# The slot loop of a hypergraph layer: four pairs of row banks, the next round's first tiles and gates made in this round, two tiles scaled on ScalarE

## The reference

```python
h = x @ W
beta = sigmoid((h @ a_gn)[:, None, :] + (agg @ a_ge)[:, :, None])
all_he = beta[..., None] * h[:, None, :, :] + (1.0 - beta[..., None]) * agg[:, :, None, :]
all_he = elu(all_he)
logits2 = where(H[None, :, :] > 0, se[:, None, :], NEG)
coefs1 = softmax(logits2, axis=-1)
g = einsum('bne,benf->bnf', coefs1, all_he)
```

## Time and profile before

| | |
|---|---|
| time, median of 3 runs | 2310.97 us (2310.77 to 2312.5) |
| profiled execution | 2305.04 us, of which the span is 2303.3 |
| VectorE busy over the span | 2034.9 us, 88% |
| TensorE matmuls | 2041.7 us, 89% |
| ScalarE | 1391.4 us, 60% |
| GpSimd | 929.2 us, 40% |
| the loop's first VectorE instruction starts at | 130.65 us |
| the next part starts at | 322.34 us |
| rounds of the loop | 9 (72 adds on GpSimd, 8 a round) |

### The profile page before, as it was taken

The page is one execution under the profiler, slowest core; times in us unless marked ns, Lnnn a source line. Parts: engine busy times, 40 slices in busy tenths (PEclk is TensorE's granted clock), DMA queues, the critical chain, the costliest instruction groups (busy, mean ns, idle before and its releaser), DMA issues. The chain is left out here.

```text
span 2303.3 us, 61385 instructions
## 1 busy us (share of the span) xinstructions
PE 2041.7 (89%) x26444; PEld 1347.3 (58%) x26444; DVE 2034.9 (88%) x2731; ACT 1391.4 (60%) x2174; POOL 929.2 (40%) x534
## 2 busy tenths in 40 slices
PE   6888866478878699999999999999999999998886
PEld 5654534345566466666666666666666666665654
DVE  7568866589757599999999999999999999999995
ACT  4422222389731466667766667766677766676784
POOL 2259950145400234444444444444444444432221
PEclk9999978678979799999999999999999999999998
DMA  3000000334300421021121211201210210123442
GB/s 126 1 0 0 0 0 1 75 62 78 48 2 1 93 53 38 30 57 39 30 47 39 52 35 39 52 25 39 52 43 30 43 43 30 34 57 60 71 71 47
DMA packets 176819, 94.74 MB, mean 41 GB/s; under 512 B 158552, under 2 KB 163864, under 8 KB 176432
## 3 DMA queue, kind: packets, MB, share of 16 engines
q1 hardware_dynamic: 176560, 90.94, 18.1%
HBM read 80.09 MB, written 10.83 MB: 39 GB/s over the span
## 5 line engine op out<-in xcount | busy, mean ns | idle before, releaser
L603 ACT ACTIVATE x_sb<-x_sb,hid_neg_max 128x1024 f32<-128x1024 f32 x576 | 661.7, 1154 | 289.7 <-DVE hid_neg_max L518 289.5
L527 DVE STREAM_TRANSPOSE hid_weights_t<-x_sb 128x1024 f32<-128x1024 f32 x576 | 712.2, 1237 | 2.7 <-ACT x_sb L603 2.3
L518 DVE CUSTOM_DVE_ANT_0 x_sb<-ps_score,adj_mask,row_scale 128x1024 f32<-128x1024 f32 x512 | 638.9, 1248 | 16.4 <-PE ps_score L386 15.3
L406 PE MATMUL ps_low<-hid_weights_t,hid_x_rep 32*64 32x256 f32 x18432 | 573.3, 382 | 11.5 <-ACT hid_share L633 11.1
L386 PE MATMUL ps_score<-hid_y_hi,hid_xs 128*128 128x512 f32 x1152 | 522.0, 453 | 34.9 <-DVE hid_neg_max L518 29.4
L406 PEld LDWEIGHTS ps_low<-hid_weights_t,hid_x_rep 32*64 32x64 f32 x18432 | 390.8, 132 | 168.4 <-issue 97.6
L386 PE MATMUL ps_score<-hid_y_lo,hid_xs 128*128 128x512 f32 x1152 | 456.6, 396 | 0.0
L713 POOL TENSOR_TENSOR hid_z<-hid_z,hid_inv_cols 128x1024 f32<-128x1024 f32 x64 | 194.5, 3040 | 553.9 <-ACT hid_z L611 553.9
L386 PEld LDWEIGHTS ps_score<-hid_y_hi,hid_xs 128*128 128x128 f32 x1152 | 217.0, 188 | 261.7 <-issue 151.1
L386 PEld LDWEIGHTS ps_score<-hid_y_lo,hid_xs 128*128 128x128 f32 x1152 | 218.4, 190 | 43.9 <-issue 15.0
L705 POOL TENSOR_TENSOR hid_y_wide<-hid_y_wide,hid_y_hi 128x1024 f32<-128x1024 f32 x64 | 153.6, 2400 | 191.5 <-ACT hid_y_wide L594 191.5
(11 more groups left out here) (350 smaller groups left out, 3058.8 us busy)
## 6 DMA issues: line engine op xcount, KB each, us to landing
hid_inv_cols<-hid_inv_rows SPq DMA_DIRECT2D x64, 512.0 KB, 3.7
hid_x_rep<-hid_row_space SPq DMA_DIRECT2D x64, 256.0 KB, 5.8
gat_x_rep<-gat_row_space SPq DMA_DIRECT2D x32, 256.0 KB, 5.7
gat_e_wide<-gat_e_space SPq DMA_DIRECT2D x8, 512.0 KB, 6.5
marks<-hid_mark_rows SPq DMA_DIRECT2D x8, 512.0 KB, 4.8
x_sb<-in_x SPq DMA_DIRECT2D x4, 512.0 KB, 5.8
hyp_neighbours<-in_adj SPq DMA_DIRECT2D x4, 512.0 KB, 7.1
edge_adj_high<-in_adj SPq DMA_DIRECT2D x4, 512.0 KB, 9.0
```

The source lines that it names most:

```text
L406: ins = pe.matmul(m.ps_low[c * F:(c + 1) * F, a, 0:NT * Q], x_rep[a * Q:(a + 1) * Q, batch_of(g) % 2, b, :], weights_t[a * Q:(a + 1) * Q, ...
L518: dve.tensor_tensor_reduce(ring[:, i % RING, :], m.ps_score[:, i % 2, :], mask, scale, HUGE, ALU.add, ALU.min, neg_max[:, g % 2, t:t + 1]) ...
L527: dve.transpose(weights_t[:, g % 2, :, t, :], ring[:, i % RING, :].rearrange("p (b j) -> p b j", j=Q)).then_inc(tile_turned, 1)
L603: act.activation(ring[:, i % RING, :], ring[:, i % RING, :], ACT.Exp, scale=-1.0, bias=neg_max[:, g % 2, t:t + 1], accum_out=row_sum[:, g ...
```

## The change

It makes the loop's rounds overlap.

- `pick` is made by comparing `rank` with `level`, a [128, 1] count that goes up by one a round, so `rank` stays as it is.
- The small products go to a part of the first row bank, and VectorE copies them to SBUF (`small`) before that bank is used for rows. The gates then read the copy.
- There are four pairs of row banks (two in `ps_score`, two in `ps_low`). TensorE makes the rows of tiles 0 to 2 of the next round at the end of this one, and the small products between `add_diff(6)` and `add_diff(7)`.
- VectorE makes `pick` after tile 4 of this round, asks for the next round's gates (`ask`, `settle_beta`) after tile 6, and ends them (`settle_coef`) after tile 7. `scale_away` of the next round's tiles 0 and 1 stands in this round. Round 0's gates and first tiles are made ahead of the loop; the last round makes a set that nobody uses, and TensorE closes those three accumulations after the loop.
- ScalarE scales the shares of tiles 1 and 3 by coef, eight small activations a tile, after the exp of the tile that follows. GpSimd then only adds these two.

```diff
--- before.py
+++ after.py
@@ -2230,7 +2230,12 @@
             diff_ready, blend_ready, blend_exped, share_ready, share_added = (
                 sem("diff_ready"), sem("blend_ready"), sem("blend_exped"),
                 sem("share_ready"), sem("share_added"))
-            small = m.ps_misc[:, 0, 0:NT * 18].rearrange("p (t c) -> p t c", t=NT)
+            act_scaled, small_taken = sem("act_scaled"), sem("small_taken")
+            level = psb("level", [P, 1])
+            next_beta = psb("next_beta", [P, NT, B])
+            small = psb("small", [P, NT, 18])
+            small_bank = m.ps_score[:, 0, 0:NT * 18]
+            ACT_TILES = (1, 3)
             block = part.enter_context(nc.Block())
 
             def along(v, t):
@@ -2241,55 +2246,86 @@
 
             def row_banks(t):
 
-                if t % 3 == 2:
-                    return m.ps_turn[:, 0, :], m.ps_turn[:, 1, :]
-                return m.ps_score[:, t % 3, 0:HALF], m.ps_score[:, t % 3, HALF:N]
+                if t % 4 >= 2:
+                    return m.ps_low[:, t % 4 * 2 - 4, :], m.ps_low[:, t % 4 * 2 - 3, :]
+                return m.ps_score[:, t % 4, 0:HALF], m.ps_score[:, t % 4, HALF:N]
 
             def slot_count(eng):
                 return eng.value_load(slots_int[0:1, 0:1], min_val=1, max_val=EN)
 
             @block.tensor
             def _(pe):
-                with pe.Fori(0, slot_count(pe)) as k:
-                    pe.wait_ge(picked, k + 1)
+                def find_small():
                     for t in range(NT):
-                        ins = pe.matmul(m.ps_misc[:, 0, t * 18:(t + 1) * 18], pick[:, t * P:(t + 1) * P],
+                        ins = pe.matmul(small_bank[:, t * 18:(t + 1) * 18], pick[:, t * P:(t + 1) * P],
                                         picks[:, B * F:], start=True, stop=True)
                     ins.then_inc(small_ready, 1)
 
...
+                def row_pair(t):
+                    row, away = row_banks(t)
+                    cols = slice(t * P, (t + 1) * P)
+                    pe.matmul(row, pick[:, cols], picks[:, 0:B * F], start=True, stop=False)
+                    pe.matmul(away, ident_r[:], h1_hi[:, t, :], start=True, stop=False)
+                    pe.matmul(away, ident_r[:], h1_lo[:, t, :], start=False, stop=False)
+                    pe.matmul(away, pick[:, cols], picks_neg[:], start=False, stop=True)\
+                      .then_inc(rows_ready, 1)
+
+                pe.wait_ge(picked, 1)
+                find_small()
+                pe.wait_ge(small_taken, 1)
+                for t in range(3):
+                    row_pair(t)
+                with pe.Fori(0, slot_count(pe)) as k:
                     def add_diff(t):
                         pe.wait_ge(diff_ready, k * NT + t + 1)
                         pe.matmul(row_banks(t)[0], m.ident[:], diff[:, t % 2, :], start=False,
                                   stop=True).then_inc(blend_ready, 1)
 
-                    for t in range(3):
+                    for t in range(5):
+                        add_diff(t)
+                        pe.wait_ge(rows_taken, k * NT + t + 4)
+                        row_pair(t + 3)
+                    add_diff(5)
+                    add_diff(6)
+                    pe.wait_ge(picked, k + 2)
+                    pe.wait_ge(rows_taken, k * NT + 9)
+                    find_small()
+                    add_diff(7)
+                    pe.wait_ge(small_taken, k + 2)
+                    row_pair(0)
+                    for t in (1, 2):
+                        pe.wait_ge(rows_taken, k * NT + 9 + t)
                         row_pair(t)
-                    for t in range(NT):
-                        add_diff(t)
-                        if 1 <= t and t + 2 < NT:
-                            row_pair(t + 2)
+                for t in range(3):
+                    pe.matmul(row_banks(t)[0], ident_r[:], h1_hi[:, t, :], start=False, stop=True)
 
             @block.scalar
             def _(act):
+                def exp_gates(n):
+                    act.wait_ge(beta_asked, n)
+                    act.activation(next_beta[:], next_beta[:], ACT.Exp, scale=-1.0).then_inc(beta_exped, 1)
+                    act.wait_ge(coef_asked, n)
+                    act.activation(coef[:], coef[:], ACT.Exp).then_inc(coef_exped, 1)
+
+                exp_gates(1)
                 with act.Fori(0, slot_count(act)) as k:
-                    act.wait_ge(beta_asked, k + 1)
-                    act.activation(beta[:], beta[:], ACT.Exp, scale=-1.0).then_inc(beta_exped, 1)
-                    act.wait_ge(coef_asked, k + 1)
-                    act.activation(coef[:], coef[:], ACT.Exp).then_inc(coef_exped, 1)
+                    def scale_share(t):
+                        if t == ACT_TILES[0]:
+                            act.wait_ge(coef_taken, k + 1)
+                        act.wait_ge(share_ready, k * NT + t + 1)
+                        s = by_batch(share[:, t % 4, :])
+                        for b in range(B):
+                            ins = act.activation(s[:, b, :], s[:, b, :], ACT.Copy, scale=pool_coef[:, t, b:b + 1])
+                        ins.then_inc(act_scaled, 1)
+
                     for t in range(NT):
                         act.wait_ge(blend_ready, k * NT + t + 1)
                         act.activation(blend_exp[:, t % 2, :], row_banks(t)[0], ACT.Exp,
                                        bias=minus_one[:, 0:1]).then_inc(blend_exped, 1)
+                        if t - 1 in ACT_TILES:
+                            scale_share(t - 1)
+                        if t == 6:
+                            exp_gates(k + 2)
 
             @block.gpsimd
             def _(pool):
@@ -2299,46 +2335,72 @@
                     pool.wait_ge(coef_ready, k + 1)
                     pool.nop().then_inc(coef_seen, 1)
                     pool.tensor_copy(pool_coef[:], coef[:]).then_inc(coef_taken, 1)
-                    pool.wait_ge(coef_taken, k + 2)
+                    pool.wait_ge(coef_taken, k + 1)
                     for t in range(NT):
-                        pool.wait_ge(share_ready, k * NT + t + 1)
                         s = share[:, t % 4, :]
-                        pool.tensor_tensor(by_batch(s), by_batch(s), along(pool_coef, t), ALU.mult)\
-                            .then_inc(scaled, 1)
-                        pool.wait_ge(scaled, k * NT + t + 1)
+                        if t in ACT_TILES:
+                            pool.wait_ge(act_scaled, k * len(ACT_TILES) + ACT_TILES.index(t) + 1)
+                        else:
+                            pool.wait_ge(share_ready, k * NT + t + 1)
+                            pool.tensor_tensor(by_batch(s), by_batch(s), along(pool_coef, t), ALU.mult)\
+                                .then_inc(scaled, 1)
+                            pool.wait_ge(scaled, k * (NT - len(ACT_TILES)) + t - sum(a < t for a in ACT_TILES) + 1)
                         pool.tensor_tensor(rows[:, t, :], rows[:, t, :], s, ALU.add)\
                             .then_inc(share_added, 1)
 
             @block.vector
             def _(dve):
...
+                def choose():
+                    dve.tensor_scalar(pick[:], rank[:], level[:, 0:1], None, ALU.is_equal).then_inc(picked, 1)
+
+                def ask(n, link):
+                    dve.wait_ge(small_ready, n)
+                    dve.tensor_copy(small[:].rearrange("p t c -> p (t c)"), small_bank).then_inc(small_taken, 1)
+                    dve.wait_ge(small_taken, n)
+                    dve.tensor_tensor(next_beta[:], small[:, :, B:2 * B], gate[:], ALU.add).then_inc(beta_asked, 1)
                     link(dve.tensor_tensor(coef[:], small[:, :, 0:B], best[:], ALU.subtract))
                     dve.scalar_tensor_tensor(out=coef[:], in0=coef[:], scalar=0.0,
                                              in1=linked[:].unsqueeze(2).to_broadcast([P, NT, B]),
                                              op0=ALU.min, op1=ALU.mult).then_inc(coef_asked, 1)
...
+                def settle_beta(n, link):
+                    dve.wait_ge(beta_exped, n)
+                    link(dve.tensor_scalar(next_beta[:], next_beta[:], 1.0, None, ALU.add))
+                    link(dve.reciprocal(beta[:], next_beta[:]))
+
+                def settle_coef(n, link):
+                    dve.wait_ge(coef_exped, n)
+                    link(dve.tensor_tensor(coef[:], coef[:], small[:, :, 16:17].to_broadcast([P, NT, B]),
+                                           ALU.mult))
+                    dve.nop().then_inc(coef_ready, 1)
+                    link(dve.tensor_tensor(coef_sum[:], coef_sum[:], coef[:], ALU.add))
+                    link(dve.tensor_scalar(level[:], level[:], 1.0, None, ALU.add))
+
+                def scale_row(t):
+                    dve.tensor_tensor(by_batch(diff[:, t % 2, :]), by_batch(row_banks(t)[1]),
+                                      along(beta, t), ALU.mult).then_inc(diff_ready, 1)
+
+                first = Chain(dve, step)
```

(43 more changed lines are left out.)

40 lines of the change are left out of this document (removed).

## The result

| | before | after |
|---|---|---|
| median of 4 runs | 2310.87 us (2308.36 to 2312.5) | 2341.62 us (2339.73 to 2345.26) |
| ratio | | 1.0136, 95% interval 1.012 to 1.0152 |
| profiled execution, span | 2305.04, 2303.3 | 2342.97, 2341.2 |
| loop's first VectorE instruction to the next part | 130.65 to 322.34: 191.7 | 131.27 to 353.55: 222.3 |
| mean period of a round | 20.58 | 23.45 |

The forecast of 2338.0 is 3.6 us from the median. The loop is 30.6 us longer in the trace, and the whole kernel 30.75 by the medians. The two profiled executions differ by more, 37.9 of span: 0.6 ahead of the loop and 6.7 behind it, in code that the change leaves alone.

The account below looks back on a forecast made before the run. VectorE was taken as the bound (13.3 of tiles, 7.3 of gates), GpSimd 0.7 behind. Eight periods 3.0 slower make 24, plus 3.4 at the end: 27 on 2310.97 gives 2338; range 2298 to 2346, the forecast's own 2326 to 2345.

Parts of the forecast that it names:

- The rule of the Trainium skill that was weighed: VectorE with two SBUF inputs contends with a GpSimd instruction reading SBUF; with one, outside two-port modes, not; gives 27 us.
- The doubt from coef_sum's 0.23: Gates: coef_sum has two SBUF inputs yet takes 0.23 under GpSimd; guessed it may just meet a gap every round.
- two such behind each other cost a whole GpSimd instruction for the second: Gates on VectorE: a two-SBUF-input instruction following another waits about 1.18, the middle of GpSimd's two pitches.
- the walk: Timeline of one changed round from its first share at 0, six gates contended, next first share at 23.6.
- TensorE's work counts for nothing either way: Rows of three first tiles made early leave the path but were covered already; nothing counted.
- The walk's choice of rows: VectorE, after scale 6 at 9.3: waits for GpSimd's add, then works 0.7, to 10.75.
- The end: After the last round VectorE still makes an unused round's gates and two scales; 3.4 us more.
- the same instructions run: Ahead of the loop, with GpSimd idle: copy 0.3 more, rank 0.5 less; put at zero.
- The 0.5 saved on rank: Ahead of the loop: rank's part costs 0.5 less, set against 0.3 more for the copy.
- Tensor_tensor does not wait: Rival on the gates: only scalar_tensor_tensor and the choice wait; round 20.59 again, 2311 (2306 to 2318); chance 0.20.
- GpSimd was the bound and the gates are hidden: Rival on the loop: round limited to 19.0, 14 us faster, 2297, at the most 2284; chance 0.22.
- That the gate exps on ScalarE hold tile 7: Rival: gate exps ahead of tile 7's exp undo the overlap; up to 1 us a round, 2347; inside forecast's upper bound.

Follow-up runs that it names:

- the first experiment: Kernel before the change, with only the small products copied from PSUM to SBUF and the gates reading the copy, no overlap; 2324.68 us, ratio 1.0064.
- the best version: Changed kernel with two-input gates keeping one in PSUM, three bank pairs, ScalarE on tiles 5 and 6, next first difference early, unread matmuls; 2295.14 us.

## Why the prediction was right, and where its terms were off

*The mechanism.* Gates that had read PSUM became held instructions under a GpSimd that is never idle then. Beta's sum and the product rose as said, and the first experiment reproduces half of the loss with the copy alone; with GpSimd light no loss is left. The rule of the Trainium skill that was weighed, page "SBUF — State Buffer", section "Who interferes with whom", agrees: with one input in PSUM the scalar_tensor_tensor stayed at 0.224 to 0.226 in 10 of 10, with two in SBUF its median was 0.50 to 1.33 in nine kernels. The doubt from coef_sum's 0.23 is settled as the prediction guessed: the same instruction took 0.79, 1.01 and 1.19 in three other orders. It had met the gap behind a multiply.

*The size of the round.* 23.6 was predicted and 23.45 measured, and that they agree so well is luck: two errors cancel. Coef's difference was put at 1.1 and took 0.21. The step at fault is "two such behind each other cost a whole GpSimd instruction for the second", taken from a pair in which the first got through behind an add. Behind a multiply the second passes too, and coef_sum's 0.23 at the end of a multiply was the row that showed it. So the walk is 0.8 late there, and 1.2 at the round's end; the short rounds are 22.4. The long ones are 1.65 longer by TensorE's clock, 1.0 on average, which the prediction had no term for; it said that TensorE's work counts for nothing either way. The walk's choice of rows, held behind GpSimd's add, was to end at 10.75 and ends at 11.16 (173.21 + 1.73, from 163.78). ScalarE's batch takes 2.0, not 1.7, and share 3, which waits 0.80 for its exp, comes 6.25 after the first and not 5.85. Level's +1 takes 0.153 and was never held; 0.2 was the guess. GpSimd's idle time was put at 5 to 6 a round, ahead of tile 1's add and of tile 7; in the short round it is 1.70 + 2.56 + 0.81 = 5.1, in the long one 1.65 + 4.22 + 0.82 = 6.7.

*The ends.* The end was put at 3.4 and is 4.2; the last round is a long one (24.1, 0.5 over the forecast's), and the 0.3 from VectorE's last instruction to the next part was left out. Ahead of the loop zero was predicted and 3.4 measured. That is the step that failed: "the same instructions run". Most of it is the clock: the small products and rows ran at the lower level, granted clock 0.50 where it was 1.00 before. The products took 1.88 for 1.06, and both scales waited for rows, 0.88 and 0.94. But not all: with unread matmuls it was 1.00 and the stretch still took 8.89 against 6.78. Of these 2.1, 1.2 are the unread matmuls' own, since the products start 2.39 into the stretch there and 1.15 into it in the kernel before. The other 0.9, an estimate from these rows, is the new order, in which the rows wait for the copy (0.40). The 0.5 saved on rank was no saving: share 0 waited 0.55 for its exp behind it in the kernel before.

*What bounds the kernel before.* The prediction called VectorE the bound and GpSimd 0.7 behind. Two experiments show this as too simple: 1.5 off VectorE's path and two multiplies off GpSimd's together gave nothing, and so did 0.7 off the gates. The two are locked: VectorE's decrement doesn't end until GpSimd's instruction has, and GpSimd waits for the share behind it. Each round was GpSimd's 19.9 plus the 0.7 of one share. And 0.9 beneath that lies a third path that the prediction counted as covered: TensorE's twelve row matmuls at the round's start, partly at the lower clock, ahead of tile 0's exp. Without the decrement that path sets share 0.

*The rivals.* "Tensor_tensor does not wait" is refuted by 1.05 and 1.19. "GpSimd was the bound and the gates are hidden" would have needed idle gates; with the gates in PSUM it comes true in part, at 2295 against its 2297, though that version also has other tiles on ScalarE, another order on TensorE and unread matmuls, so the agreement says little. That the gate exps on ScalarE hold tile 7 was not seen: in the round of 163.78 share 7 starts behind the scale at 181.99 with no wait.

Left open: why the clock fell when it did, since the length of the idle stretch doesn't tell it (below); how much of the loss ScalarE's tiles make by themselves; and what unread matmuls alone bring in the best version, which was not tried without them.

## What to carry to other kernels

Under a busy GpSimd, a small VectorE instruction with two inputs in SBUF, or a +1 on 64 elements from SBUF to SBUF, costs what is left of the GpSimd instruction under way: 0.2 becomes up to 1.3 us. The reciprocal and the +1 on one element were never held. In a chain each link can pay; whether the next one does depends on whether GpSimd pauses behind the instruction that let the first through. Keep one input of each in PSUM, the intermediate results too, rather than copy them to SBUF: reading PSUM in place of the copy gave 28 us in the changed kernel (together with three pairs of banks), and moving two more results there gave 15 by itself. And don't add up savings that end in a held instruction. The two tried here, of 0.7 and 1.5 a round, brought nothing, because the instruction behind them was held or another path came in.
